# Splitting a block-diagonal product over the two halves of TensorE's rows in a CIN and tower kernel

## What is computed

```
e  = 39 table rows per sample                         # [b, 39, 16]
Xi = e
for W, b in three layers:                             # H = 128
    Xi = einsum('hjk,bjd,bkd->bhd', W, e, Xi) + b
    res.append(Xi.sum(axis=2))                        # sum over d
h = concat(res, dense_ctx)                            # [b, 3*128 + 16]
y = relu(relu(h @ W_top1 + b1) @ W_top2 + b2) @ W_top3
```

## Time and profile before

| | |
|---|---|
| median of 3 runs | 696.32 us (695.7 to 696.78) |
| the profiled execution: its own time | 697.1 us |
| its span | 695.2 us |
| mean granted TensorE clock | 0.993 |
| TensorE matmuls busy | 651.2 us (94%) |
| VectorE busy | 566.9 us (82%) |
| GpSimd busy | 444.2 us (64%) |
| ScalarE busy | 410.4 us (59%) |

### The profile page before, as it was taken

The page is one execution under the profiler, slowest core; times in us unless marked ns, Lnnn a source line. Parts: engine busy times, 40 slices in busy tenths (PEclk is TensorE's granted clock), DMA queues, the critical chain, the costliest instruction groups (busy, mean ns, idle before and its releaser), DMA issues.

```text
span 695.2 us, 10601 instructions
## 1 busy us (share of the span) xinstructions
PE 651.2 (94%) x2856; PEld 495.7 (71%) x2856; DVE 566.9 (82%) x1495; ACT 410.4 (59%) x1369; POOL 444.2 (64%) x372
## 2 busy tenths in 40 slices
PE   0079999999999999999999999999999999999997
PEld 0046777777778777777778877777778777777767
DVE  4039999999994599999995589999997479999980
ACT  3025767666663466767673476767674366767751
POOL 6746777777783377777775367777775366454440
PEclk9999999999999999999999999999999999999999
DMA  6246424040403103122221201313030300300000
GB/s 214 49 128 232 151 60 122 6 124 6 124 7 105 24 3 88 43 64 68 58 75 42 83 7 37 95 28 103 18 114 17 99 16 18 111 1 6 0 2 1
DMA packets 39055, 44.33 MB, mean 64 GB/s; under 512 B 17427, under 2 KB 22253, under 8 KB 38867
## 3 DMA queue, kind: packets, MB, share of 16 engines
q1 hardware_dynamic: 33363, 42.34, 20.0%
q0 software_dynamic: 5632, 1.31, 2.1%
HBM read 8.86 MB, written 0.00 MB: 13 GB/s over the span
## 4 chain that ended last, share of the span: by engine, by line
PE 88%; POOL 4%; DVE 3%; DMA 2%; issue 2%; SPq 1%; ACT 1%; POOLq 0%; DVEq 0%
PE p_u L541 20%; PE p_u L542 20%; PE p_u L543 20%; PE p_x L518 13%; PE p_tower L560 5%; PE p_g L551 5%; POOL emb L257 3%; DVE parts L449 1%; DVE x2t L457 1%; PE p_tower L587 1%; PE p_tower L573 1%; DMA emb<-table_in,idx_all 1%; PE p_tower L572 1%; PE p_tower L579 1%; PE p_x L508 1%
## 5 line engine op out<-in xcount | busy, mean ns | idle before, releaser
L331 ACT ACTIVATE prod<-p_u,x0t 128x128 f32<-128x128 f32 x1024 | 290.9, 369 | 140.4 <-PE p_u L543 140.1
L449 DVE SCALAR_TENSOR_TENSOR parts<-p_u,x0t,parts 128x128 f32<-128x128 f32 x1024 | 283.7, 343 | 50.4 <-PE p_u L543 50.3
L541 PE MATMUL p_u<-w1h,x1h 128*128 128x512 f32 (+1 forms) x640 | 303.9, 475 | 4.1 <-DVE x1l L426 2.3
L542 PE MATMUL p_u<-w1l,x1h 128*128 128x512 f32 (+1 forms) x640 | 250.4, 391 | 0.0
L543 PE MATMUL p_u<-w1h,x1l 128*128 128x512 f32 (+1 forms) x640 | 250.2, 391 | 0.0
L273 POOL TENSOR_TENSOR parts<-parts,prod 128x512 f32<-128x512 f32 x128 | 173.1, 1353 | 77.6 <-ACT prod L331 66.3
L257 POOL DMA_INDIRECT emb<-table_in,idx_all x176 | 181.3, 1030 | 51.2 <-issue 47.8
L541 PEld LDWEIGHTS p_u<-w1h,x1h 128*128 128x128 f32 x640 | 120.9, 189 | 52.6 <-issue 20.4
L268 POOL TENSOR_TENSOR parts<-prod 128x512 f32<-128x512 f32 x64 | 89.6, 1400 | 99.6 <-ACT prod L331 99.3
L542 PEld LDWEIGHTS p_u<-w1l,x1h 128*128 128x128 f32 x640 | 121.5, 190 | 42.8 <-issue 20.2
L543 PEld LDWEIGHTS p_u<-w1h,x1l 128*128 128x128 f32 x640 | 120.7, 189 | 25.8
(11 more groups left out here) (46 smaller groups left out, 204.6 us busy)
## 6 DMA issues: line engine op xcount, KB each, us to landing
fac_b<-xx SPq DMA_DIRECT2D x96, 234.0 KB
fac_a<-xx SPq DMA_DIRECT2D x48, 78.0 KB
emb<-table_in,idx_all POOLq DMA_INDIRECT x176, 2.5
g_all<-w_in SPq DMA_DIRECT2D x3, 832.0 KB, 9.8
xx<-xx SPq DMA_DIRECT2D x32, 78.0 KB
fac_b<-xx SPq DMA_DIRECT2D x16, 156.0 KB
w<-w_in SPq DMA_DIRECT2D x1, 2496.0 KB, 10.3
bd<-x0t SPq DMA_DIRECT2D x128, 10.0 KB, 2.1
```

The source lines that it names most:

```text
L331: last = nc.scalar.activation(dst[:, i * H:(i + 1) * H], u[:, i * H:(i + 1) * H], ACT.Copy, scale=x0t[:, par, t, j:j + 1])
L449: nc.vector.scalar_tensor_tensor(out=chain[:, p, i, :], in0=u[:, i * H:(i + 1) * H], scalar=x0t[:, par, t, j:j + 1], in1=add, op0=ALU.mult ...
L541: nc.tensor.matmul(u, xh, wh, start=True, stop=False)
L542: nc.tensor.matmul(u, xh, wl, start=False, stop=False)
```

## The change

The block-diagonal product is cut in two. Partitions 0 to 63 hold the tile's samples 0 to 3 and partitions 64 to 127 samples 4 to 7, and the rest of `bd` is zero; so the 160 columns of samples 0 to 3 need only the upper 64 rows, and the other 160 only the lower 64. The two products stand on different halves of the array's rows (`tile_position` (0, 0) and (64, 0)) and write to two banks, `p_g` and `p_tower`. `keep_g` becomes two copies. Since `p_tower` is also the tower's bank, waits are added on TensorE, and `tower_3` moves from slot 35 to slot 36.

```
-S_Z3, S_Z3_STEP, S_Z3_OUT, S_H1, S_H2, S_Y = 15, 5, 23, 26, 31, 35
+S_Z3, S_Z3_STEP, S_Z3_OUT, S_H1, S_H2, S_Y = 15, 5, 23, 26, 31, 36
+HALF_B = TILE_B // 2
...
+        g_banks = (p_g, p_tower)
...
             def keep_g(T, tt):
                 act.wait_ge(g_full, T + 1)
-                nc.scalar.activation(g_all[:, :, TILE_B * tt:TILE_B * (tt + 1)],
-                                     p_g[:, 0:TILE_B * GJ].rearrange("h (b j) -> h j b", j=GJ),
-                                     ACT.Copy).then_inc(g_kept, 1)
+                for i in range(2):
+                    b = TILE_B * tt + HALF_B * i
+                    nc.scalar.activation(g_all[:, :, b:b + HALF_B],
+                                         g_banks[i][:, 0:HALF_B * GJ].rearrange("h (b j) -> h j b", j=GJ),
+                                         ACT.Copy).then_inc(g_kept, 1)
...
             def tower_z(n):
-                act.wait_ge(g_kept, TILES_BLOCK * (n + 1))
+                act.wait_ge(g_kept, 2 * TILES_BLOCK * (n + 1))
...
             def layer2(T, tt, pair, par):
-                need(pe, g_kept, T)
-                nc.tensor.matmul(p_g[:, 0:TILE_B * GJ], x2t[:, p, :], bd[:, par, t].rearrange("p b j -> p (b j)"),
-                                 start=True, stop=True).then_inc(g_full, 1)
+                need(pe, g_kept, 2 * T)
+                for i in range(2):
+                    r = slice(64 * i, 64 * i + 64)
+                    last = nc.tensor.matmul(g_banks[i][:, 0:HALF_B * GJ], x2t[r, p, :],
+                                            bd[r, par, t, HALF_B * i:HALF_B * (i + 1)].rearrange("p b j -> p (b j)"),
+                                            start=True, stop=True, tile_position=(64 * i, 0))
+                last.then_inc(g_full, 1)
...
             def tower_z3(n, j0, j1):
                 if j0 == 0:
-                    pe.wait_ge(g_kept, TILES_BLOCK * (n + 1))
+                    pe.wait_ge(g_kept, 2 * TILES_BLOCK * (n + 1))
                     pe.wait_ge(w2_in, 16)
+                if j0 == 0 and n < BLOCKS - 1:
+                    pe.wait_ge(g_kept, 2 * (TILES_BLOCK * (n + 1)))
...
                         if q == Q_LAYER2 and (has_prev or tt > 1):
+                            if has_prev and m == 0 and s > S_Z3_OUT:
+                                pe.wait_ge(z3_made, 2 * n)
+                            if has_prev and m == 0 and s > S_H2:
+                                pe.wait_ge(h2_made, C2 * n)
+                            if has_prev and m == 1  and s < QUADS:
+                                pe.wait_ge(y_made, n)
                             layer2(T - 2, (tt - 2) % TILES_BLOCK, n * (MACROS // 2) + mm // 2, mm % 2)
...
                             if s == S_H1:
                                 pe.wait_ge(z3_made, 2 * n)
+                                pe.wait_ge(g_kept, 2 * (TILES_BLOCK * n + 1))
...
                             if s == S_Y:
+                                pe.wait_ge(g_kept, 2 * (TILES_BLOCK * n + 2))
                                 tower_3(n - 1)
```

## The result

The changed kernel takes 706.69 us (median of 4 runs, 705.18 to 709.09), the kernel before 696.55 us (4 runs) beside it: ratio 1.0149, 95% interval 1.0132 to 1.0167, so +10.1 us. The forecast was 718.7 us (+22.4). The time lies in the range of 705 to 726, the direction is right, and the size is wrong by more than a factor of two. 705.9 us had been the figure of the rival "halves fully side by side, changes paid", with a chance of 12%; the range began at 705 to hold it.

What follows compares the result with a forecast made beforehand. TensorE, streaming without gaps in the loop, was taken as the bound, VectorE 4% behind. 58 tiles x 0.33 us (19.1) + 3.2 for slot 24 + 0.1 in the tail = 22.4 us on 696.3, giving 718.7 us; range 705 to 726.

Steps and rivals of the forecast that it cites:

- halves fully side by side, changes paid: Rival for each tile's product: halves run at once, row changes cost; +0.11 us x 58 + 3.2 = 9.6, 705.9 us; chance 12%.
- TensorE bounds the loop, every 0.1 us in a tile counts: Loop: TensorE streams without gaps, so each tenth gained or lost in a tile is in the time, until VectorE takes over.
- A change of rows costs 0.19 us, 64 rows like 16: Each tile: going from 128 rows to 64 and back costs 2 x 0.19 = 0.38 us, taken from 128/16-row products.
- What the halves stream: Each tile's product: four instructions of 0.135 us; only the middle two can overlap, saving 0.135 us, or 0.05 by loads.
- The term -0.05 us: Saving in each tile from the halves' overlap, limited by weight loads at one in 0.11 us.
- the bound of -0.27: Other bound in each tile: halves fully side by side take 0.27 us, saving 0.27.
- 58 tiles, since the last macro's wait swallows four: Of 62 products in the loop, four in the last macro hide under a 0.43 us wait; 58 x 0.33 = 19.1 us.
- Slot 24: 1.05 us, three times: Macro 0 of three blocks: TensorE waits for ScalarE's read of p_tower, 1.05 us each, 3.2 us in all.
- Slot 36, 15, 26, 34 and ScalarE's 11 us: nothing: Waits in these slots covered or at most 0.1 us each; ScalarE's longer copies, 11 us, hidden except 0.1 in the tail.
- The clock: Rival: with slot 24's wait, half clock could fall in all three towers or elsewhere; +3 to +6 us, 722 to 725; chance 6%.
- The rival that ended faster: Rival for each tile: 64 rows cost no change, saving 0.135 to 0.27 us; 691.7 or 683.8 us; chance 10%.

Runs made afterwards that it cites:

- split_slots: Changed kernel with the two halves issued in two slots, half 0 before quad 4 and half 1 before quad 5; 753.30 us, ratio 1.0774 to the kernel before.
- full_rows: Changed kernel, but both 160-column products read all 128 rows; banks, copies and waits stay; 707.25 us, ratio 1.0108 to the kernel before.
- one_half: Changed kernel with only the first half computed, ScalarE copying the first bank twice; 711.38 us, ratio 1.0171 to the kernel before.
- slot24_whole: Changed kernel, but slot 24 of each block's first macro uses the old 128-row product into p_g; 709.07 us, ratio 1.0108 to the kernel before.

## Why the prediction was wrong, step by step

- **TensorE bounds the loop, every 0.1 us in a tile counts.** Right: 0.12 us in a tile came out as 7.4 us.
- **A change of rows costs 0.19 us, 64 rows like 16.** Right: 0.38 us for both (split_slots), and full_rows brings the tile back to 1.01.
- **What the halves stream.** This step failed. The prediction said: "A product's two instructions stand one after the other and use the same rows, so in order of issue only the second of half 0 and the first of half 1 can lie side by side", and, that "the four weight loads bound it too". Neither holds. The two products' instructions interleave: both first ones start within 0.01 us, then both second ones, and the loads for different halves of rows run at once too. The term -0.05 us measured some -0.26 (the halves' streams take 0.27 us and the second half adds 0.01, one_half, where 0.54 would be in turns). The pace of one load in 0.11 us was read from loads to the same rows; the rows held no case of two different halves, and the bound of -0.27 that stood beside it was nearly the value. With it, the sum would have been 58 x 0.11 + 3.2 + 0.1 = 9.7 us, which is the measured size (10.1). That the time lies in the stated range is owed to this rival, not to the forecast's own working.
- **58 tiles, since the last macro's wait swallows four.** Wrong, by 0.5 us. The period there grew by 0.12 like elsewhere. TensorE and VectorE wait for each other there: the longer product delays the quad for which VectorE waits (0.73 us, before 0.61), VectorE frees the bank that much later, and TensorE's 0.43 us stay.
- **Slot 24: 1.05 us, three times.** Right; slot24_whole takes it away, and it isn't made up for.
- **Slot 36, 15, 26, 34 and ScalarE's 11 us: nothing.** Right: the only wait for the copies that costs TensorE time is that of slot 15, which was there before (1.8 us in all, 1.4 after). In slot 36 the profile names the copies as what ended the idle time, but `tower_3`'s load starts 0.33 us after the last product of `quad` (244.41 to 244.74), as it did before without such a wait (0.32).
- **The clock.** The rival said that the wait in front of slot 26 would make it fall in all three towers. It fell in none of those in the loop in the profile after. Over eleven profiles with the old order of the tower's first layer (33 blocks' towers in the loop) half clock shows in 9; in the three with the new order (9 towers) in none. The runs' mean clock is 0.002 to 0.003 higher with the new order than with the old in each of three pairs. That the order is the cause is likely but not shown; nine cases are few.

The rival that ended faster needed both changes of rows together to cost under 0.21 us in a tile; they cost 0.38.

## What to carry to other kernels

Two products on different halves of the array's rows really run at once, loads and all, but coming from and going back to full rows costs some 0.38 us, here more than the 0.27 us saved. So pack only where enough small products stand together for one visit; two tiles' products in one visit took 0.95 us of TensorE instead of 1.08, and even that lost here, as VectorE had no time to spare. Order neighbours by their number of rows first: splitting one loop in two took 3.5 us (0.5%) out of the stream here, and the medians fell by 0.7 to 0.9% together with a higher clock, whose cause is not shown. When a trace offers one bound for "in turns" and one for "at once" and holds no case of either, keep both as forecasts rather than reason one away by the order of issue.

## What was not expected of the hardware

- Two fp32 products on rows 0 to 63 and 64 to 127 start 0.01 us apart although each is two instructions with two loads; on the same 64 rows the second starts 0.37 us after the first (0.11 of it for the first load).
- VectorE's product of two tensors in SBUF takes 0.69 us alone, and took 1.31 us where GpSimd's addition of two tensors had started 0.5 us before it; the other way round GpSimd's takes 1.81 instead of 1.3. So a shift in time can make an engine slower that has no part in the change. The Trainium skill, "SBUF — State Buffer", SBUF: two separate sides, says that the port pair shared by a VectorE instruction with two SBUF inputs and a GpSimd one that reads SBUF is an exclusive lock, which whoever starts first holds for its whole instruction. The trace agrees nearly: the product at 129.21 ends 0.55 us after GpSimd's addition (129.97), where one held up altogether would end 0.69 after.
